# A dot, a subtraction and a batch's moments change their places in an attention and expert kernel

## The reference

```python
# x, ctx: (16, 256, 256), f32
x = x + tanh(g_xattn) * xattn(ctx, layernorm(x))
x = x + tanh(g_ffn) * moe(layernorm(x))

def xattn(media, latents):             # 8 heads of 128
    xn, ln = layernorm(media)*g+b, layernorm(latents)*g+b
    q  = ln @ Wq + bq                                  # 256 queries
    kv = concat([xn, ln]) @ Wkv + bkv                  # 512 keys
    return softmax(q k^T / sqrt(128)) v @ Wo + bo

def moe(x):                            # 8 experts, F = 1024, top 2
    w, idx = top_k(x @ Wg + bg, 2); w = softmax(w)
    return sum_k w_k * (silu(x @ W1[idx_k] + b1[idx_k]) @ W2[idx_k] + b2[idx_k])
```

## Time and profile before

| | |
|---|---|
| median of 3 runs | 1505.71 us (1504.64 to 1506.18) |
| profiled execution | 1498.99 us, span 1497.3 us |
| TensorE busy | 1464.5 us (98%) |
| VectorE busy | 1223.7 us (82%) |
| ScalarE busy | 942.0 us (63%) |
| GpSimd busy | 580.1 us (39%) |

### The profile page before, as it was taken

One profiled execution on the slowest core, in us unless ns is written; L12 is line 12 of the kernel. 1 busy time (PEld: TensorE's weight loads), 2 busy tenths in 40 slices (PEclk: granted clock), 3 DMA queues, 4 the chain that ended last, 5 costly groups with the idle time before them and its releaser, 6 DMA issues. The chain is left out here.

```text
span 1497.3 us, 29981 instructions
## 1 busy us (share of the span) xinstructions
PE 1464.5 (98%) x10138; PEld 1345.8 (90%) x10138; DVE 1223.7 (82%) x3169; ACT 942.0 (63%) x2047; POOL 580.1 (39%) x650
## 2 busy tenths in 40 slices
PE   8999999999999999999999999999999999999997
PEld 6888888888888888888988888988899999999996
DVE  7879989898898989989898998787767766666685
ACT  5665655656556555655656556556668877777775
POOL 4323324242332424324243333333444555445542
PEclk9999999999999999999999999999999999999998
DMA  6210101101110110101101010032556555555563
GB/s 200 57 36 15 43 22 41 53 16 43 23 36 22 51 43 15 44 22 46 48 16 44 23 36 22 8 98 70 111 153 195 157 132 134 145 145 128 132 184 76
DMA packets 83491, 107.99 MB, mean 72 GB/s; under 512 B 24297, under 2 KB 68390, under 8 KB 83086
## 3 DMA queue, kind: packets, MB, share of 16 engines
q1 hardware_dynamic: 67374, 87.03, 18.2%
q0 software_dynamic: 15824, 18.98, 7.9%
q10 hardware_dynamic: 144, 0.05, 0.0%
HBM read 87.68 MB, written 18.35 MB: 71 GB/s over the span
## 5 line engine op out<-in xcount | busy, mean ns | idle before, releaser
L973 POOL TENSOR_SCALAR probs<-probs,rsum 128x512 f32<-128x512 f32 x256 | 182.4, 724 | 636.2 <-DVE rsum L1696 630.1
L1197 ACT ACTIVATE pt_hi<-turn 128x512 fp32r<-128x512 f32 x256 | 139.0, 595 | 228.3 <-PE turn L1356 226.8
L999 POOL DMA_INDIRECT out_rows<-yo,token x71 | 127.6, 1797 | 188.5 <-DVE yo L1872 168.6
L1821 DVE TENSOR_TENSOR ht_lo<-hs,ht_hi 128x512 fp32r<-128x512 f32 x142 | 98.3, 692 | 116.1 <-ACT ht_hi L1164 112.9
L1096 ACT ACTIVATE probs<-score,nbias 128x512 f32<-128x512 f32 x256 | 172.8, 684 | 1.9 <-DVE nbias L1692 1.8
L1155 ACT ACTIVATE hs<-ph,vecs 128x256 f32<-128x256 f32 (+1 forms) x284 | 114.2, 457 | 94.5 <-PE ph L199 84.1
L1948 DVE TENSOR_TENSOR pt_lo<-turn,pt_hi 128x512 fp32r<-128x512 f32 x256 | 164.0, 682 | 3.9 <-ACT pt_hi L1197 3.5
L1690 DVE TENSOR_REDUCE smax<-score 128x1 f32<-128x512 f32 x256 | 164.0, 679 | 2.9 <-PE score L199 2.7
L197 PE MATMUL py<-w_hi,ht_lo 128*128 (+1 forms) x568 | 162.8, 287 | 3.2 <-DVE ht_lo L1821 1.7
L198 PE MATMUL py<-w_lo,ht_hi 128*128 (+1 forms) x568 | 161.0, 284 | 0.6 <-issue 0.5
L199 PE MATMUL py<-w_hi,ht_hi 128*128 (+1 forms) x568 | 160.8, 283 | 0.0
(11 more groups left out here) (251 smaller groups left out, 4746.5 us busy)
## 6 DMA issues: line engine op xcount, KB each, us to landing
w_raw<-in_L_ffn_W SPq DMA_DIRECT2D x45, 1024.0 KB, 5.4
spread<-mean_and_factor SPq DMA_DIRECT2D x15, 512.0 KB
xhat_rows<-rows SPq DMA_DIRECT2D x16, 264.0 KB, 2.2
x_raw<-in_x SPq DMA_DIRECT2D x16, 256.0 KB, 3.0
c_raw<-in_ctx SPq DMA_DIRECT2D x16, 256.0 KB, 3.2
out_rows<-x SPq DMA_DIRECT2D x16, 256.0 KB
z_turned<-in_x_turned SPq DMA_DIRECT2D x15, 256.0 KB, 3.8
z_turned<-in_ctx_turned SPq DMA_DIRECT2D x15, 256.0 KB, 4.5
```

The lines of the kernel that those rows point to most:

```text
L973: last = pool.tensor_scalar(probs[n % 2][:, t, :], probs[n % 2][:, t, :], rsum[:, n % 2, t:t + 1], 1.0, ALU.mult, ALU.mult)
L999: pool.indirect_dma_start(out=A["out"], out_offset=bass.IndirectOffsetOnAxis(ap=token[:, u:u + 1].bitcast(U32), axis=0), in_=yo_of(t)[:, s ...
L1197: act.activation(pt[0][:, 2 * t:2 * t + 2, :], turn[t][:, :].rearrange("p (j i) -> p j i", j=2), ACT.Copy).then_inc(s_pthi, 1)
L1821: dve.tensor_tensor(lo[:, :], hs[n % N_HS][:, :], hi[:, :].bitcast(F32), ALU.subtract).then_inc(s_hlo, 1)
```

## The change

It has five parts. (1) The constant `LIST_TILES` grows from 32 to 34, so the experts' lists begin 17 KB apart instead of 16 KB. (2) The third warm-up has 5 transposes instead of 8. (3) `split_kv` is cut in two, `round_kv` (rounding) and `rest_kv` (subtraction); at step 3 of a batch `prepare` stands between them. For batch 1 they stay together. (4) GpSimd waits for the first normalised rows (`s_z`) before it makes the first weights' low parts. (5) On VectorE one dot of step 4 moves to step 3, where it stands ahead of `kt_lo` (the dots are renumbered, 5 in step 3, 5 in step 4, 6 in step 5, instead of 4, 6 and 6), and the moments of batch 1 are computed in two halves inside step 0: the first behind `kt_lo`, the second before the last `v_lo`, instead of both at its end.

```diff
-LIST_TILES = TOKENS // P
+LIST_TILES = TOKENS // P + 2
...
-WARM_UP = 20, 3, 8, 6
+WARM_UP = 20, 3, 5, 6
...
-            def split_kv(c):
+            def round_kv(c):
 
                 pool.wait_ge(s_zt, c)
                 if c >= 2:
 
                     pool.wait_ge(s_full, number["q", H * (c - 1) - 1] + 1)
                     pool.wait_ge(s_full, number["v", (2 * (c - 2) + 1, JT - 1)] + 1)
+                own.mark(pool.tensor_copy(kvt[c % 2][0][:, :, :], zt[:, :, :]))
+
+            def rest_kv(c):
                 hi, lo = kvt[c % 2]
-                own.mark(pool.tensor_copy(hi[:, :, :], zt[:, :, :]))
                 own.wait()
                 pool.tensor_tensor(lo[:, :, :], zt[:, :, :], hi[:, :, :].bitcast(F32), ALU.subtract)\
                     .then_inc(s_kvt, 1)
...
+            pool.wait_ge(s_z, 1)
             lo_weights(pool, "pool", "q0", "k0", "k1")
...
                 if i == 4:
-                    split_kv(1)
+                    round_kv(1)
+                    rest_kv(1)
                 if h == Z_STEP and 1 <= b < B - 1:
-                    split_kv(b + 1)
+                    round_kv(b + 1)
                 if h == A_STEP and b + 2 < B:
                     prepare(b + 2)
+                if h == Z_STEP and 1 <= b < B - 1:
+                    rest_kv(b + 1)
...
-                if summed and h == G_STEP:
-                    dots(b - 1, 4, 5)
+                if summed and h == T_STEP:
+                    dots(b - 1, 0, 1)
...
                     if u[0] == "k":
+                        if i == 0:
+                            prepare_a(1, 0)
...
                         if summed and h == T_STEP:
-                            dots(b - 1, 0, 3)
+                            dots(b - 1, 1, 4)
...
                 for u in steps[i]:
+                    if i == 0 and u == [v for v in steps[0] if v[0] == "v"][-1]:
+                        prepare_a(1, 1)
 
                     if u[0] == "o" and summed and h == T_STEP:
-                        dots(b - 1, 3, 4)
+                        dots(b - 1, 4, 5)
...
                 if i == 0:
                     lo_weights(dve, "dve", "q1")
-                    prepare_a(1)
```

## The result

The changed kernel takes 1488.42 us (median of 5 runs, 1487.90 to 1488.66), the kernel before, run beside it, 1504.64 us (5 runs, 1503.71 to 1506.18). The profiled execution has a span of 1486.7 us and a time of 1488.42; before it was 1497.3 and 1498.99.

A forecast was written before the change was run, and what follows sets the result against it. TensorE is busy nearly throughout; its main loss was taken as late kt_lo, 0.64 us per batch in thirteen batches. The sum 7.8 + 0.7 + 0.9 = 9.4 us takes the median from 1505.7 to 1496.3 us, range 1493.5 to 1501.5.

The forecast's parts named there:

- Part 1: Head step 4, batches 1 to 13: subtraction after prepare frees nbias, so kt_lo comes earlier; 7.8 us, 8.3 if engines share.
- The 0.04 us taken off for the dots: Per-step deduction from 0.64 us, because blocked dots would bring the normalisation within 0.1 us of TensorE's transposes.
- Part 2: Dot moved from step 4 to step 3: matters only if the subtraction's move fails; alone up to 0.34 x 13 = 4.4 us.
- rival (c): Step 4: moved subtraction slips by 0.87 us and delays the transposes; no change, 1507.0 us, chance 0.10.
- Parts 3 and 4: Kernel start: GpSimd waits for first rows, 0.7 us; batch 1's moments move into step 0 pauses, 0.9 us.
- Part 3: Kernel start: GpSimd's wait for the first rows lets z end earlier; 0.7 us, between 0 and 0.95.
- Part 5: Experts' lists 17 KB apart: same DMAs, other addresses, TensorE never waits for them; 0, at most 1 us either way.
- The step from the profile to the median: Median before stood 6.7 us above the profiled execution; the same 9.4 us was subtracted from both, giving 1496.3.
- Rivals: Four alternatives: about half the main gain lost, 0.17; start gives nothing, 0.08; no change, 0.10; slower, 0.05.

The follow-up runs named there:

- kv_only: Kernel before with only the subtraction moved behind prepare: 1512.03 us, ratio 1.0042.
- lists_kv_dot: Kernel before with lists 17 KB apart and the subtraction and the dot moved, start and moments as before: 1484.84 us, ratio 0.9925.
- set 1: Follow-up runs on one chip, each the kernel before with one part of the change; kernel before beside them 1505.8 us.
- lists_only: Kernel before with only the lists moved to 17 KB apart: 1499.34 us, ratio 0.9963.
- set 3: Follow-up runs on the second chip varying list distance and doubling the list writes, against the kernel before at 1502.6 us.
- no_lists_again: Changed kernel with lists left 16 KB apart, rerun beside the changed kernel: 1493.62 us, 0.9938 of the kernel before.
- after_again: The changed kernel, nothing altered, measured again on the second chip: 1486.38 us, 0.9896 of the kernel before.
- set 2: Follow-up runs on the second chip: changed kernel with other list distances or without a part, against the kernel before at 1495.0 us.
- no_lists: Changed kernel with lists left 16 KB apart, first run: 1484.36 us, 0.9922 of the kernel before.
- dot_only: Kernel before with only the dot moved from step 4 to step 3: 1510.87 us, ratio 1.0037.
- twice_16: Changed kernel with lists 16 KB apart and each batch's four list writes made a second time: 1510.59 us, 1.0057 of the kernel before.
- set 4: Follow-up runs on a third chip: list writes moved, ScalarE's program shifted, batch 1's split earlier, changed kernel again; kernel before 1516.9 us.

## Why the prediction was wrong, point by point

**Part 1, the subtraction behind prepare: right, slightly undersized.** Forecast 7.8, measured 13 x 0.64 = 8.3 us. The subtraction started 2.1 us behind the step's start (forecast 2.2), kt_lo 3.2 (3.2), nbias took 0.17. The 0.04 us taken off for the dots did not come: the first of them stood, for half a microsecond, the rest took 0.42, and the normalisation starts 6.1 us behind the step's start where 6.3 were forecast. qt_lo starts 0.91 us behind the subtraction's end, where the forecast had 1.05, and the subtraction ended 0.1 us sooner.

**Part 2, the dot: the number right, the sentence wrong.** "It matters only if part 1 fails" is refuted by kv_only (step 9.18 us, 6.3 us slower in all) beside lists_kv_dot (7.90). The working of part 1 put kt_lo "no longer behind a dot" and so used part 2 without counting it. The statement that nothing on VectorE between the bias and kt_lo has two SBUF inputs, which stood against rival (c), is true only with the dot moved. As both edits are in the change, the sum did not suffer. The lock that the Trainium skill states (SBUF — State Buffer, "SBUF: two separate sides") agrees with kv_only: the dot started 0.39 us behind GpSimd's 2.40 us subtraction and ended only 0.29 us behind it.

**Parts 3 and 4, the start: right, part 3 less surely.** Forecast 0.7 and 0.9, measured 0.84 and 0.94 us in the two traces. The 0.94 stands in every trace (8.80 to 8.83 us without the moments' move, 7.84 to 7.88 with it). Part 3 scatters: the first transposes come at 24.36 to 25.36 us in the five traces with the old start (mean 25.05) and at 24.32 to 24.92 in the thirteen with the new one (mean 24.59), 0.46 us apart. In kv_only, which has the old start, GpSimd's subtraction happened to start at 7.56 and each z took 0.41. In the changed kernel GpSimd's subtraction of Q's weights waited 0.85 us for z, and both z take 0.73 together. nbias of step 1 was held up as forecast, to 1.05 us, but by less than was won ahead of it.

**Part 5, lists 17 KB apart: the step that failed.** It said "Same number of DMAs, other addresses. The one wait on them is GpSimd's 3.42 us ... 0, at most 1 us either way". Measured alone: 6.4 us in set 1 (lists_only), 7.2 in set 3 (no_lists_again against after_again), 1 to 2 in set 2. It looked only for engines that wait for the list writes by name. The 3.42 us wait was itself the sign: in that trace the last write, of 512 bytes, landed 7.2 us behind its issue, and the prediction didn't ask why. What slow writes cost stands under other names: a load of other data (x_raw, `spread`), or signals of TensorE that come late and show as "remote" or "issue", and then TensorE's granted clock. The Trainium skill has a rule that bears on it (DMA: Bandwidth & Descriptors, "🔬 Latency and other measured facts", the row on HBM row pitch): copies whose rows lie 4 MB apart ran at 103 GB/s, and 4 KB more brought back 214. At its smallest distance, 512 KB, it still has 207, so it didn't name this case. The landing records here show late writes for lists 16 and 32 KB apart, and half a KB of pad was enough.

**The step from the profile to the median.** The prediction said that the median before is 6.7 us above its profiled execution and took the same 9.4 off both. That gap was no constant of the measurement. The likely reading is that it was luck in the profiled execution, which had 1.7 us of long steps, while in the experiments traces with 16 KB and one set of writes have between 1.9 us (no_lists) and 18.5 us (dot_only) of them. Spans say 10.6 us, medians 16.2, and the changed kernel has no gap. The parts add up, though they come from different sets: 6.4 (lists_only) + 8.3 + 1.8 = 16.5 us against 16.2. No trace here is of a slower execution of the kernel before, so this reading of the gap is argued, not shown.

**Rivals.** None of the four came about. (c) feared a moved subtraction that collides. kv_only shows one, but not as (c) had it: the subtraction kept its 2.40 us, and it was the dot ahead of kt_lo that stood, in a kernel without part 2.

## What to carry to other kernels

Move an operation on GpSimd past an exclusive use of the SBUF ports only after listing every VectorE instruction in the new window, and the ones queued behind them. When small scattered writes to DRAM go to tables a power of two apart, pad the tables first and count later: what they cost does not show under their own name. When a pause ends with no work in sight, read when the signal came that ends it, before blaming the engine that pauses. And when medians lie above the profiled execution and scatter by tens of microseconds, look for steps that are long in one trace and not in the next, before forecasting from the one trace at hand.

## What the hardware showed that was not expected

- Words written to lists 16 or 32 KB apart land 5 to 22 us behind the last issue, at 16.5 or 17 KB 4 to 8 us, though their packets, read from 192 to 199 us, took 9 to 15 ns each in either case.
- While they are outstanding, a load of 256 KB takes up to 9.6 us to land in place of 3.0, and TensorE's signals come late: ScalarE, which waits for one, pauses for up to 10.6 us, as its timeline in twice_16 shows (TensorE's signal came at 290.62):

```profile
290.64 0.69 ACT L1114 ACTIVATE kt_hi<-ring,vecs 128x512 fp32r<-128x512 f32 x1 [10.60 <-remote]
```

- The Trainium skill (Runtime: NRT & Kernel Launch, "🔬 Instruction fetch mechanics") says that an engine fetches its next block while it runs the present one and that the cost of crossing into it is mostly hidden. The traces with 17 KB agree, for none has a single long step; whether it also holds with slow writes outstanding, no run here settles.
- Behind TensorE's stop of 2.43 us in no_lists_again the granted clock was half for 6.8 us. In dot_only it was half for 3.4 us behind each of TensorE's waits of 2.60 and 4.43 us (from 338.3 and from 601.2).
- After its longest step, no_lists_again ran steps of 7.93 us in place of 7.90 to the end of the attention, some 3 us in all, with the granted clock at 1.00 again. Why is open.
- Why slow writes cost 1 to 2 us in set 2 and over 7 in set 3, with the same landings and on the same chip, is open too. In set 4 the kernel before was 34 us slower than the changed one, with granted clocks of 0.991 to 0.995 against 0.997 to 0.998.
